# Selective scan with a mixture of experts: units by halves of the channels, and small VectorE work moved to GpSimd and ScalarE

## What is computed

```python
x  = layernorm(x)                                   # per token
# the recurrent branch: 256 channels d, 16 states s, rank 64
xz = rms(x) * norm_w @ W_in;  xi, z = split(xz)
xc = silu(causal_conv4(xi) + conv_b)
dt, B, C = split(xc @ W_x)
dt = softplus(dt @ W_dt + b_dt)
h[t,d,s] = exp(dt*A[d,s]) * h[t-1,d,s] + dt*xc*B[t,s]
y = sum_s(h * C) + D_skip * xc
s = x + (y * silu(z)) @ W_out
# the experts: 8 of them, the best 2 of each token count
p = softmax(x @ Wg);  scores = top2(p) / sum(top2(p))
g = silu(sum_e scores_e * (relu(x @ W1_e + b1_e) @ W2_e + b2_e))
out = x_input + s * g
```

## Time and profile before

| | |
|---|---|
| median of 3 runs (lowest, highest) | 395.79 us (393.49, 396.25) |
| the profiled execution: its own time | 393.58 us |
| its span, first to last instruction | 391.6 us |
| granted TensorE clock, mean over the span | 0.873 |
| busy: DVE, PE, POOL, ACT | 314.6, 287.7, 228.1, 214.2 us |

### The profile page before, as it was taken

The page is one execution under the profiler, slowest core; times in us unless marked ns, Lnnn a source line. Parts: engine busy times, 40 slices in busy tenths (PEclk is TensorE's granted clock), DMA queues, the critical chain, the costliest instruction groups (busy, mean ns, idle before and its releaser), DMA issues. The chain is left out here.

```text
span 391.6 us, 4141 instructions
## 1 busy us (share of the span) xinstructions
PE 287.7 (73%) x1191; PEld 147.4 (38%) x1191; DVE 314.6 (80%) x374; ACT 214.2 (55%) x405; POOL 228.1 (58%) x197
## 2 busy tenths in 40 slices
...
DMA packets 16755, 26.74 MB, mean 68 GB/s; under 512 B 4263, under 2 KB 9758, under 8 KB 16734
## 3 DMA queue, kind: packets, MB, share of 16 engines
...
## 5 line engine op out<-in xcount | busy, mean ns | idle before, releaser
L358 POOL TENSOR_TENSOR hc<-hs,Ct 128x512 f32<-128x512 f32 x126 | 160.2, 1295 | 72.3 <-DVE hs L735 72.3
L735 DVE TENSOR_TENSOR_SCAN hs<-dec,pdbu 128x1024 f32<-128x1024 f32 x64 | 146.2, 2284 | 4.5
L448 ACT ACTIVATE dec<-rep,negA 128x512 f32<-128x512 f32 x128 | 88.6, 722 | 42.3 <-DMA rep<-dt_u 30.6
L726 DVE TENSOR_TENSOR pdbu<-rep,pB 128x1024 f32<-128x1024 f32 x64 | 78.5, 1227 | 32.3 <-PE pB L816 21.1
L908 PE MATMUL px<-xnT,w 128*128 128x512 f32 x128 | 71.8, 668 | 17.2 <-ACT hT L542 13.6
L914 PEld LDWEIGHTS px<-w,hT 128*128 128x128 f32 x512 | 68.3, 212 | 29.0 <-issue 12.3
L914 PE MATMUL px<-w,hT 128*128 128x128 f32 x512 | 70.9, 298 | 9.5 <-DVE glc L669 7.5
L411 POOL TENSOR_TENSOR acc<-acc,ysc 128x512 f32<-128x512 f32 x29 | 37.5, 1292 | 47.7 <-ACT ysc L531 38.8
L542 ACT ACTIVATE hT<-px,cols 128x512 f32<-128x512 f32 x64 | 43.7, 689 | 22.5 <-PE px L908 19.1
L531 ACT ACTIVATE ysc<-px,score 128x128 f32<-128x128 f32 x116 | 33.1, 367 | 39.5 <-PE px L914 36.7
L837 PE MATMUL py<-hc,rsel 128*32 128x512 f32 x256 | 47.5, 668 | 8.2 <-POOL hc L358 8.2
...
## 6 DMA issues: line engine op xcount, KB each, us to landing
rep<-dt_u SPq DMA_DIRECT2D x128, 128.0 KB, 2.4
...
```

The source lines that it names most:

```text
L358: eng.tensor_tensor(hc[:, n % HC_RING, i, :], hs[:, n % HS_RING, i, :], Ct[:, k % 2, j, :], ALU.mult).then_inc(hc_last if n == UNITS - 1 e ...
L448: act.activation(dec[:, n % DEC_RING, i, :], rep[:, q, 0, :], ACT.Exp, scale=negA[:, q, j:j + 1])\
L726: dve.tensor_tensor(pdbu[:, :, :], rep[:, 2 * pair:2 * pair + 2, 1, :], pB[:, :, :].to_broadcast([P, 2, CH]), ALU.mult).then_inc(dbu_done, 1)
L735: dve.tensor_tensor_scan(hs[:, n % HS_RING].rearrange("p b t -> p (b t)"), dec[:, n % DEC_RING].rearrange("p b t -> p (b t)"), pdbu[:, :, ...
```

## The change

- **Order of the units.** A chunk now runs its first 128 channels through all four quads (8 units), then the second 128. Hence `py` needs one bank, and `skip_xc` and `gate_y` are done once for each half (`gate_y` at slots 20 and 36 where it was 35). The bank that is freed goes to `pB`: B of a quad is spread once for each half, 32 times where it was 16, into two banks in turn, one spread ahead. Each half of `dt_u` is copied as soon as it is ready. Job `o` starts its first half behind the first `gate_y`.
- **Rows' scaling.** `scale_rows` and `normalise` of chunks 1 to 3 go from DVE to ACT (with offsets computed once by POOL). Those of chunk 0 stay on DVE.
- **Softplus.** ACT adds 1 to e (tile `plus`), between exp and log; the correction is then one DVE instruction.
- **Gate.** `gp`, `gif`, `gvn`, `gw` and `score` go to POOL in three steps (`gate_probs`, `gate_shares`, `gate_scores`); `goh` becomes one instruction on DVE, `gs2` a reduction. DVE waits for POOL twice on the way. ACT's and PE's users of the scores wait for POOL. `gs` and `gb` move from slots 21 and 22 to 30 and 31 (for chunk 0 from 5 to 6), `y0` and `y1` of chunk 0 from 4 and 6 to 7 and 9.

The diff, cut to its core (left out: declarations, the old forms of `normalise` and `scale_rows` on DVE, which stay for chunk 0 alone, and where loops call the moved steps; in ACT's loop they stand behind `silu` and ahead of the banks' emptying, in POOL's loop the gate's steps stand behind `times_C` and `softplus_sum`):

```diff
 PRE_JOBS = ["tr", "xc0", "xc1", "dt", "v0", "v1", "tn", "m0a"]
-EARLY = {0: ["m1a", "gl", "z0"], 2: ["m0b", "z1"], 3: ["m1b"], 5: ["gs"], 6: ["gb"]}
+EARLY = {0: ["m1a", "gl", "z0"], 2: ["m0b", "z1"], 3: ["m1b"], 6: ["gs", "gb"]}
 FIRST = {
-    4: ["y0"], 5: ["tr"], 6: ["z1", "y1", "xc0<"], 8: ["xc0"], 9: ["m3a"], 10: ["xc1<"], 12: ["z0", "xc1"],
+    5: ["tr"], 6: ["z1", "xc0<"], 7: ["y0"], 8: ["xc0"], 9: ["y1", "m3a"], 10: ["xc1<"], 12: ["z0", "xc1"],
     13: ["m2b", "m2a", "dt", "tn"], 15: ["v0", "v1"], 17: ["gl", "m3b"], 18: ["y2"], 19: ["y3"],
...
     16: ["m1a", "m0a"], 17: ["m1b", "tn"], 18: ["y0", "gl"], 19: ["m2a"], 20: ["m2b", "y1"],
-    21: ["m3a", "gs"], 22: ["m3b", "gb", "y2", "m4a"], 23: ["y3"], 24: ["m4b"], 26: ["m5b"],
-    27: ["y4", "m5a"], 28: ["m6b"], 30: ["m6a"], 31: ["m7a"], 32: ["y5"], 33: ["y6", "m7b"], 35: ["o"],
+    21: ["m3a"], 22: ["m3b", "y2", "m4a"], 23: ["y3"], 24: ["m4b"], 26: ["m5b"],
+    27: ["y4", "m5a"], 28: ["m6b"], 30: ["m6a", "gs"], 31: ["m7a", "gb"], 32: ["y5"], 33: ["y6", "m7b"], 35: ["o"],
     36: ["y7"],
...
 STEPS = [{
-    "silu": [13], "log1p": [15, 15], "correct": [16, 16, 16, 16], "sum_dt": [15, 15], "times_dt": [18, 21],
-    "scale_rows": [4], "normalise": [14], "gate": [19, 20, 20, 20, 21, 21], "gate_e": [19], "gate_y": [35],
+    "silu": [13], "log1p": [15, 15], "correct": [16, 16], "sum_dt": [15, 15], "times_dt": [18, 21],
+    "scale_rows": [4], "normalise": [12], "gate": [19, 20, 23, 23, 26], "gate_e": [19], "gate_p": [21, 24, 27], "gate_y": [20, 36],
 }, {
-    "silu": [12], "log1p": [15, 15], "correct": [16, 16, 17, 19], "sum_dt": [16, 20], "times_dt": [18, 21],
-    "scale_rows": [4], "normalise": [11], "gate": [19, 20, 20, 20, 20, 20], "gate_e": [20], "finish": [20],
-    "gate_y": [35],
+    "silu": [12], "log1p": [15, 15], "correct": [16, 17], "sum_dt": [16, 20], "times_dt": [18, 21],
+    "scale_rows": [4], "normalise": [11], "gate": [19, 20, 23, 23, 26], "gate_e": [19], "gate_p": [21, 24, 27], "finish": [20],
+    "gate_y": [20, 36],
 }]
-START = {"gate": [1, 1, 1, 3, 3, 3], "gate_e": [0]}
-END = {"gate_y": [35]}
+START = {"gate": [1, 1, 3, 3, 5], "gate_e": [0], "gate_p": [1, 3, 5]}
+END = {"gate_y": [20, 36]}
 LEAD = 2
...
-    return n // PER_CHUNK, n // PAIRS % QUADS, n % PAIRS
+    k, b = n // PER_CHUNK, n // PER_HALF % DB
+    return k, n // HALF_PAIRS % QUADS, HALF_PAIRS * b + n % HALF_PAIRS
...
-        pB = banks("pB", 1)
+        pB = banks("pB", 2)
         pdbu = banks("pdbu", 2)
-        py = banks("py", DB)
+        py = banks("py", 1)
         px = [banks(f"px{i}", 1)[:, 0, :] for i in range(AUX)]
...
+                sp.wait_ge(far_done, DB * k + pair // HALF_PAIRS + 1)
                 if k > 0:
-                    free = PER_CHUNK * (k - 1) + PAIRS * (QUADS - 1) + pair + 1
+                    b = pair // HALF_PAIRS
+                    free = PER_CHUNK * (k - 1) + PER_HALF * (b + 1) - HALF_PAIRS + pair % HALF_PAIRS + 1
                     sp.wait_ge(decay_done, 2 * free)
...
                 pool.tensor_tensor(rstd[:, t], ve[:, t], mhalf[:, t], ALU.pow).then_inc(ln_rstd, 1)
+                if g == 0:
+                    return
+                pool.wait_ge(rms_r, g + 1)
+                pool.tensor_scalar(me[:, t], mv[:, t, 0], -1.0, None, ALU.mult).then_inc(rms_me, 1)
+                pool.wait_ge(rms_me, g + 2)
+                pool.tensor_tensor(off_r[:, t], me[:, t], rr[:, t], ALU.mult).then_inc(off_done, 1)
+                pool.wait_ge(ln_rstd, g + 1)
+                pool.tensor_tensor(off_n[:, t], me[:, t], rstd[:, t], ALU.mult).then_inc(off_done, 1)
...
                                    x_sb[:, c].rearrange("p t d -> p (t d)"), ALU.add).then_inc(o_done, 1)
+
+            def gate_probs(k):
+
+                pool.wait_ge(gate_step, GATE_STEPS * k + 3)
+                pool.tensor_tensor(gp[:, :, :], gex[:, :, :], gri[:, :, None].to_broadcast([P, TPC, EXPERTS]), ALU.mult)\
+                    .then_inc(gate_pool, 1)
+
+            def gate_shares(k):
+
+                pool.wait_ge(gate_step, GATE_STEPS * k + 7)
+                pool.tensor_copy(gif[:, :, :], gi8[:, :, 0:2]).then_inc(gate_pool, 1)
+                pool.tensor_tensor(gvn[:, :, :], gv8[:, :, 0:2], grs[:, :, None].to_broadcast([P, TPC, 2]), ALU.mult)\
+                    .then_inc(gate_pool, 1)
+
+            def gate_scores(k):
+
+                pool.wait_ge(gate_step, GATE_STEPS * (k + 1))
+                pool.wait_ge(gate_pool, GATE_POOL * k + 3)
+                pool.tensor_tensor(gw[:, :, :, :], goh[:, :, :, :],
+                                   gvn.rearrange("p t j -> p j t")[:, :, :, None].to_broadcast([P, 2, TPC, EXPERTS]),
+                                   ALU.mult).then_inc(gate_pool, 1)
+                pool.wait_ge(gate_pool, GATE_POOL * k + 4)
+                pool.tensor_tensor(score[:, k % 2], gw[:, 0], gw[:, 1], ALU.add).then_inc(gate_pool, 1)
...
                 act.wait_ge(e_done, DB * k + b + 1)
+                act.activation(plus[:, b, :], ev[:, b, :], ACT.Identity, bias=one[:, 0:1]).then_inc(plus_done, 1)
                 act.activation(lg1p[:, b, :], ev[:, b, :], ACT.Ln, bias=1.0).then_inc(l_done, 1)
+
+            def normalise(k):
+
+                act.wait_ge(off_done, 2)
+                for i in range(TPC):
+                    t = TPC * k + i
+                    last = act.activation(xn[:, k, i, :], x_sb[:, k, i, :], ACT.Identity, scale=rstd[:, t:t + 1],
+                                          bias=off_n[:, t:t + 1])
+                last.then_inc(ln_xn, 1)
+
+            def scale_rows(k):
+
+                act.wait_ge(off_done, 2)
+                act.wait_ge(dt_done, DB * k)
+                for i in range(TPC):
+                    t = TPC * k + i
+                    last = act.activation(xr[:, i, :], x_sb[:, k, i, :], ACT.Identity, scale=rr[:, t:t + 1],
+                                          bias=off_r[:, t:t + 1])
+                last.then_inc(rms_xr, 1)
...
                 link(dve.reciprocal(gri[:, :], gsm[:, :]))
-                link(dve.tensor_tensor(gp[:, :, :], gex[:, :, :], gri[:, :, None].to_broadcast(wide), ALU.mult))
                 yield
+                dve.wait_ge(gate_pool, GATE_POOL * k + 1)
                 for i in range(TPC):
...
                 link(last)
+                link(dve.tensor_reduce(gs2[:, :], gv8[:, :, 0:2], AX.X, ALU.add))
+                link(dve.reciprocal(grs[:, :], gs2[:, :]))
                 yield
-                link(dve.tensor_copy(gif[:, :, :], gi8[:, :, 0:2]))
-                link(dve.tensor_tensor(gs2[:, :], gv8[:, :, 0], gv8[:, :, 1], ALU.add))
-                link(dve.reciprocal(grs[:, :], gs2[:, :]))
-                link(dve.tensor_tensor(gvn[:, :, :], gv8[:, :, 0:2], grs[:, :, None].to_broadcast([P, TPC, 2]), ALU.mult))
-                yield
-                for j in range(2):
-                    last = dve.tensor_tensor(goh[:, j], iota8[:, :, :], gif[:, :, j:j + 1].to_broadcast(wide), ALU.is_equal)
-                link(last)
-                for j in range(2):
-                    last = dve.tensor_tensor(gw[:, j], goh[:, j], gvn[:, :, j:j + 1].to_broadcast(wide), ALU.mult)
-                link(last)
-                link(dve.tensor_tensor(score[:, k % 2], gw[:, 0], gw[:, 1], ALU.add))
+                dve.wait_ge(gate_pool, GATE_POOL * k + 3)
+                wide = [P, 2, TPC, EXPERTS]
+                link(dve.tensor_tensor(goh[:, :, :, :], iota8[:, None, :, :].to_broadcast(wide),
+                                       gif.rearrange("p t j -> p j t")[:, :, :, None].to_broadcast(wide), ALU.is_equal))
                 assert n[0] == GATE_STEPS * (k + 1), n[0]
...
-            def correction(k, b, i):
-
-                if i == 0:
-                    dve.wait_ge(e_done, DB * k + b + 1)
-                    dve.tensor_scalar(corr[:, b, :], ev[:, b, :], 1.0, -1.0, ALU.add, ALU.add).then_inc(round_done, 1)
-                    return
-                dve.wait_ge(round_done, DB * k + b + 1)
-                dve.tensor_tensor(corr[:, b, :], corr[:, b, :], ev[:, b, :], ALU.subtract).then_inc(corr_done, 1)
+            def correction(k, b):
+
+                dve.wait_ge(plus_done, DB * k + b + 1)
+                dve.scalar_tensor_tensor(corr[:, b, :], plus[:, b, :], 1.0, ev[:, b, :], ALU.subtract, ALU.subtract)\
+                    .then_inc(corr_done, 1)
...
                 dve.tensor_tensor(dt_u[:, b, 1, :], dt_u[:, b, 0, :], xc[:, k % 2, b], ALU.mult).then_inc(u_done, 1)
-                if b == DB - 1:
-                    dve.wait_ge(u_done, DB * (k + 1))
-                    dve.memset(dt_u[:, :, 0, 0:CH:SEQ], FAR).then_inc(far_done, 1)
+                dve.wait_ge(u_done, DB * k + b + 1)
+                dve.memset(dt_u[:, b, 0, 0:CH:SEQ], FAR).then_inc(far_done, 1)
...
                 k, j, pair = place(n)
-                dve.wait_ge(B_spread, n // PAIRS + 1)
+                m = n // HALF_PAIRS
```

(103 more changed lines are left out.)

34 lines of the change are left out of this document (11 added, 23 removed).

## The result

The changed kernel takes 372.28 us in the median (371.49 to 373.73, 4 runs) against 395.7; the ratio is 0.942, interval 0.938 to 0.947. Its profiled execution took 371.49 with a span of 369.7, so 22.1 us less than the one of before.

A forecast was written before the change was run, and what follows sets the result against it. DVE was taken to bound E to T, a PE and ACT chain T to E; -4.0 - 1.4 - 0.8 - 13.5 + 1.0 = -18.7 from 393.58 gave 374.9, plus 2.2 for the median: 377, range 362 to 391.

The forecast's parts named there:

- the likeliest case: The forecast itself: 367 to 384 us with 377 as its middle, chance 0.55.
- The chain bounds T to E: Between T and E, PE and ACT's sequence from `tr` through convolution, silu, `dt`, `v0` to exp limits; gains 1.4 and 0.8.
- T: Cut point in each chunk where `gate_y` starts after the scan of slot 35 in the kernel before.
- E: Cut point in each chunk where DVE meets the first exp of softplus, slot 16.
- Start to E: From kernel start to the first E, 95.8 us before: gain 4.0, bounds 0 and 10.
- E to T: Three stretches where DVE is the limit and each of its instructions counts: gain 24.8 less 11.3 of new waits, 13.5.
- The correction: DVE's softplus step at E: two instructions of 0.55 and 0.91 become one of 0.9, twice a chunk, 1.2 us.
- POOL's queue: DVE waits in slots 21 and 23 of chunks 1 and 2 behind POOL's 9.1 us of work; 3.3 together taken.
- The port rule of the Trainium skill: DVE and GpSimd share ports under an exclusive lock; a DVE instruction with two SBUF inputs stands still while GpSimd reads.
- the worst case: All six merged corrections held for one whole POOL instruction each: 7.8 us back, time 385 instead of 377.
- The end: Last T to the kernel's end: later second-half `gate_y` and half of `o`, less the half done early, +1.0 us.

## Why the prediction was right, and where it was not

377 was forecast and 372.28 measured, within the range of the likeliest case. What bounds each stretch was right. That the number came so close is in part luck: the sum left out a gain of 4.7 (the late slots of `gs` and `gb`) and a cost of 3 to 4.5 (ACT's `plus`), which nearly cancel.

- *The chain bounds T to E.* Right. From `tr` to E it was 28.6 before and is 167.31 - 137.27 = 30.0 and 249.58 - 219.49 = 30.1. The growth of 0.9 was put too low by 0.5. `tr` stands 4.0 and 5.2 us behind T (4.0 and 6.1 were forecast). The run with `normalise` back on DVE shows it best: the time stays, the wait shrinks.
- *Start to E.* 4.0 forecast, 5.2 measured. The first product came 3.0 us earlier (3.3), the gate's sum at 43.70 (43.9), `gs` at 56.09 (56). From there to E it took 34.6, where 35.8 was forecast.
- *E to T.* 13.5 forecast, 16.0 measured, but the term was composed wrongly. It credited 9.2 us to B's second bank. The waits for `pB` did fall from 9.2 to nothing in these stretches, but the bank is not the only thing that does it: with one bank they are 2.9 in the new order of units and 0.24 in the old one, both with the gate moved and `gs` late. With two banks, the gate on DVE and PE standing 11.1 us at an early `gs`, there are none either. So the second bank is enough, and so, but for 0.24 to 2.9 us, is the moved gate with a late `gs`; the new kernel with both undone wasn't run, so that the 9.2 can't be shared out. What the runs price is the gate's rework, 9.3 (the sum had 13.8 less 6.6 of waits for POOL), and the later slots of `gs` and `gb`, 4.7, measured on the kernel with the gate on DVE, for which the sum had no term.
- *The correction.* It was booked as a gain of 1.2 a chunk less 1.7 in chunk 0 and 0.6 on the chain, about nothing in the sum. It costs 3 to 4.5. What failed is the price of ACT's instruction: I counted it ahead of DVE alone and took the rest as hidden in ACT's idle 45%, where in the trace it stands ahead of `hT`.
- *POOL's queue.* 3.3 us of waits in each of chunks 1 and 2 were taken for slots 21 and 23; the trace has 2.07 + 1.33 = 3.4 in chunk 1 and 2.06 + 1.33 in chunk 2. Right.
- *The port rule of the Trainium skill* (page "SBUF — State Buffer", section "Who interferes with whom"). The later corrections took 0.69, 0.86, 0.69, 1.18, 0.69 and 1.19, so they were held for some 1.2 us in all, not for the 7.8 of the worst case. Of the tiny gate instructions above, those with two SBUF inputs agree with the rule: the two `gw` took 2.43 us while POOL ran two instructions of 1.27, and ended 0.04 us behind them; a reciprocal, with one input, took 0.18 in the middle of one. The cast has one input too, and took 1.31 beside one of POOL's of 1.26; the rule as it is told here doesn't cover that.
- *The end.* +1.0 forecast, +1.1 measured. With the old order of units the last stretch is 71.3 (71.2 before), which points to the order as what costs it.
- *The parts together.* From the undone parts: gate 9.3, slots of gs and gb 4.7, rows' scaling 4.0, order and banks 8.7, correction -4.5; the sum is 22.2, against 23.4 for all at once. By the ratios, each against the kernel before in its own set, it is 26.8 against 22.9. The parts add up roughly; that they are independent isn't shown, and for the two that each remove B's waits, above, it is doubtful.

Open is what the whole chain would give if it came earlier in an order made for it: the runs that slid it moved other waits as well.
